# A memory-attention layer rebuilt: denominators from segment sums, query divided first, heads on column tiles

## What is computed

```python
def step(carry, inp):                       # over 8 segments of L = 32 tokens, per sequence and head (H = 8, DK = DV = 64)
    mem, z = carry                          # start: zeros, and ones / DK
    q_s, k_s, v_s = inp
    sq = elu(q_s) + 1.0
    att_mem = sq @ mem / (sq @ z)
    sk = elu(k_s) + 1.0
    mem = mem + einsum('bhlk,bhlv->bhkv', sk, v_s)
    z = z + sk.sum(over the segment's tokens)
    att_dot = softmax(q_s @ k_s.T * DK ** -0.5)     # within the segment
    att = gate * att_mem + (1.0 - gate) * (att_dot @ v_s)
    return (mem, z), att
s = att @ Wo
h = gelu(xn @ W_fc_ternary.T); h = layernorm(h) * ln_w + ln_b       # 512 features
g = h @ W_proj_ternary.T
x = x + s * silu(g)
```

## Time and profile before

| | |
|---|---|
| median of 3 runs | 3093.98 us (3093.51 to 3094.66) |
| the profiled execution | 3093.26 us; its span, from the first to the last instruction, 3091.5 us |
| busy in the span | PE 2651.5 us (86%), DVE 2365.2 (77%), ACT 1580.9 (51%), POOL 318.3 (10%) |
| mean granted TensorE clock | 0.864 of 2.4 GHz |
| layer 0, first to last update of x | 110.2 to 655.9 us |

### The profile page before, as it was taken

One profiled execution on the slowest core, in us unless ns is written; L12 is line 12 of the kernel. 1 busy time (PEld: TensorE's weight loads), 2 busy tenths in 40 slices (PEclk: granted clock), 3 DMA queues, 4 the chain that ended last, 5 costly groups with the idle time before them and its releaser, 6 DMA issues. The chain is left out here.

```text
span 3091.5 us, 56965 instructions
## 1 busy us (share of the span) xinstructions
PE 2651.5 (86%) x19564; PEld 2068.0 (67%) x19564; DVE 2365.2 (77%) x6278; ACT 1580.9 (51%) x3260; POOL 318.3 (10%) x340
## 2 busy tenths in 40 slices
PE   1999999979999999987764898888888889888887
PEld 1888887867777777765553666656666666656665
DVE  2777777768878888868526788888888888888887
ACT  1333334336555666555333556566565556556554
POOL 0000000000000000003321111111111111111111
PEclk9999999989999999989785777777778777777777
DMA  7000000000000000011021344323334344323334
GB/s 210 1 0 0 0 0 0 0 0 1 1 1 1 1 1 0 1 32 55 26 58 61 90 103 103 88 76 85 94 85 104 93 100 103 96 76 81 91 85 114
DMA packets 86520, 163.69 MB, mean 53 GB/s; under 512 B 18856, under 2 KB 45616, under 8 KB 86320
## 3 DMA queue, kind: packets, MB, share of 16 engines
q0 software_dynamic: 20480, 62.93, 10.7%
q1 hardware_dynamic: 64640, 98.15, 9.8%
q10 hardware_dynamic: 1200, 0.27, 0.1%
HBM read 92.60 MB, written 9.99 MB: 33 GB/s over the span
## 5 line engine op out<-in xcount | busy, mean ns | idle before, releaser
L1104 ACT ACTIVATE b_neg<-b_neg,b_nmax 128x128 f32<-128x128 f32 (+1 forms) x512 | 190.9, 443 | 207.9 <-DVE b_nmax L1258 207.9
L2770 DVE TENSOR_TENSOR_SCAN d_state<-w,d_state 128x1024 f32<-128x1024 f32 x128 | 291.0, 2284 | 6.2 <-issue 5.9
L2507 ACT ACTIVATE d_probs<-l_bank,w_b 128x256 f32<-128x256 f32 x512 | 210.7, 469 | 155.8 <-PE l_bank L2345 153.3
L2345 PE MATMUL l_bank<-xnT,w_w 128*128 128x256 f32 x1024 | 245.1, 382 | 14.0 <-ACT d_probs L2507 14.0
L2356 PEld LDWEIGHTS l_bank<-w_w,d_probs 128*128 128x128 f32 x2048 | 244.9, 192 | 11.7 <-ACT d_probs L2507 5.3
L2356 PE MATMUL l_bank<-w_w,d_probs 128*128 128x128 f32 x2048 | 252.7, 276 | 0.0
L2275 PE MATMUL l_bank<-w 9*128 9x256 f32 x1040 | 208.3, 669 | 25.6 <-ACT w L2430 18.9
L2469 ACT ACTIVATE w<-d_delta,d_negA 128x255 f32<-128x255 f32 x520 | 220.3, 499 | 0.0
L96 POOL TENSOR_TENSOR ln_rstd<-ln_var_eps,minus_half 128x2 f32<-128x2 f32 x50 | 63.9, 1278 | 1482.2 <-DVE ln_var_eps L90 1482.2
L2345 PEld LDWEIGHTS l_bank<-xnT,w_w 128*128 128x128 f32 x1024 | 184.7, 190 | 40.7 <-ACT d_probs L2507 20.9
L2275 PEld LDWEIGHTS l_bank<-w 9*128 9x128 f32 x1040 | 123.3, 320 | 96.0 <-issue 32.3
(11 more groups left out here) (404 smaller groups left out, 6110.2 us busy)
## 6 DMA issues: line engine op xcount, KB each, us to landing
d_bct<-l_bc SPq DMA_DIRECT2D x132, 512.0 KB, 3.9
d_state<-d_state POOLq DMA_DIRECT2D x96, 512.0 KB, 6.5
d_state<-d_state POOLq DMA_DIRECT2D x32, 256.0 KB, 3.8
x_sorted<-x SPq DMA_DIRECT2D x1, 2560.0 KB, 16.5
w<-in_L_ffn_w_dram SPq DMA_DIRECT2D x1, 2048.0 KB, 9.4
w_w<-in_L_ffn_W_dram SPq DMA_DIRECT2D x1, 2048.0 KB
c2e_xg<-x_sorted SPq DMA_DIRECT2D x16, 128.0 KB, 2.3
y_sorted<-c2e_yo SPq DMA_DIRECT2D x16, 128.0 KB, 1.8
```

Of the source, the lines that this page charges most:

```text
L1104: done = nc.scalar.activation(neg[:, slot, cols], neg[:, slot, cols], ACT.Exp, bias=nmax[:, slot, a:a + 1], scale=-1.0)
L2345: done = nc.tensor.matmul(bank[:, b, i * T:(i + 1) * T], w.w1[:, e, k * P:(k + 1) * P], x1T[:, :], start=True, stop=True)
L2507: done = v.activation(hid[:, e % 2, k, :], bank[:, b, i * T:(i + 1) * T], ACT.Gelu, bias=w.b1[:, e, k:k + 1])
L2770: done = v.tensor_tensor_scan(group, dA[i][:, g % (NG - 1), :, :].rearrange("p m t -> p (m t)"), group, 0.0, ALU.mult, ALU.add)
```

## The change

Only `layer0` and its constants are touched.

- Denominators: VectorE sums the positive keys over each segment (`tensor_reduce`), a scan adds the segments up from 1/64 (`tensor_tensor_scan`), the positive queries are multiplied by that sum, and TensorE sums over the 64 features of each head with a block matrix of ones (`denominators`). ScalarE inverts: Ln, then Exp of the negative (`invert`). VectorE divides the positive queries by it (`share_q`) ahead of the memory's scores. The scores, thus the output, are then divided already. `zrow`, the ones column, `share_memory` and `combine` go.
- Softmax: the probabilities are divided by their sum before they are transposed.
- Memory's scores are computed for both heads of a pair next to each other on two 64-row tiles; one mask instruction of 2 x 384 columns covers both.
- Output: `heads_out` takes values as the stationary operand (64 columns of the array per head, the two heads of a pair on the two column tiles) and scores or probabilities as the moving one, and sums memory's and softmax's parts in one bank, already transposed. `turn_attention` goes.
- Work on other engines: q and k are clipped on ScalarE (relu of -x, from PSUM); the hidden layer's normalisation moves from VectorE to ScalarE (`apply_norm`), with one more GpSimd product for its bias.
- ScalarE's function tables are loaded by hand: gelu with tanh, and exp with ln, in turn; four loads per iteration.
- `pos`, `vdot`, `vmem` and `xnT` get two buffers, the loop runs over pairs of sequences, and the values, the sums and the divided queries of sequence n+1 are made in iteration n.

The new parts, cut: the denominators, the scores and the output, the order of TensorE's loop body, and two parts of ScalarE. In that order `hidden` waits for `shifted_ready`, `turn_hidden` for the normalised hidden layer.

```diff
+            def denominators(m, half):
+                pe.wait_ge(qz_ready, 2 * m + half + 1)
...
+                for i in range(2):
+                    done = nc.tensor.matmul(bank[:, DEN, i * T:(i + 1) * T], c.head_block[:, :], qz[:, 2 * half + i, :],
+                                            start=True, stop=True)
...
+            def memory_scores(n, par, j):
+                pe.wait_ge(posq_ready, 2 * n + j // 2 + 1)
+                pe.wait_ge(mem_masked, NCH0 * n + j + 1)
+                for lo, keys in ((0, slice(0, P)), (P, slice(P, T))):
+                    for odd in range(2):
+                        rows = slice(DK0 * odd, DK0 * odd + DK0)
+                        done = nc.tensor.matmul(bank[:, MEM + odd, 2 * lo:2 * lo + T - lo], pos[rows, par, j, 1, keys],
+                                                pos[rows, par, j, 0, lo:], start=True, stop=True,
+                                                tile_position=(DK0 * odd, 0))
...
+            def heads_out(n, par, j):
+                if j == 0:
+                    pe.wait_ge(probs_ready, n + 1)
+                    pe.wait_ge(v_taken, TILES * n + TILES)
+                if j % 2 == 0:
+                    pe.wait_ge(attT_copied, 2 * n + j // 2 + 1)
+                pe.wait_ge(mem_masked, NCH0 * n + j + 2)
+                cols = slice(j % 2 * T, j % 2 * T + T)
+                for step in range(4):
+                    for odd in range(2):
+                        hd = 2 * j + odd
+                        out = bank[DK0 * odd:DK0 * (odd + 1), OUT, cols]
+                        v = slice(hd * DK0, (hd + 1) * DK0)
+                        if step == 0:
+                            left, right = vmem[:, par, 0, v], memT[:, j % 2, odd, 0:T]
+                        elif step == 1:
+                            left, right, out = vmem[:, par, 1, v], memT[:, j % 2, odd, T:], out[:, P:]
+                        else:
+                            a = step - 2
+                            left, right = vdot[:, par, a, v], probsT[:, odd, a * (H0 // 2) + j, :]
+                            out = out[:, a * P:(a + 1) * P]
+                        done = nc.tensor.matmul(out, left, right, start=(step == 0), stop=(step == 3),
+                                                tile_position=(0, DK0 * odd))
...
+                    memory_scores(n, par, 0)
+                    own_scores()
+                    memory_scores(n, par, 1)
+                    for a in range(TILES):
+                        hidden(n, par, a)
+                    turn_x(n + 1)
+                    project_qk(n + 1, 1 - par, 0)
+                    project_qk(n + 1, 1 - par, 1)
+                    project_qk(n + 1, 1 - par, 2)
+                    project_qk(n + 1, 1 - par, 3)
+                    heads_out(n, par, 0)
+                    memory_scores(n, par, 2)
+                    for a in range(TILES):
+                        turn_hidden(n, a)
+                    heads_out(n, par, 1)
+                    memory_scores(n, par, 3)
+                    for a in range(TILES):
+                        project_v(n + 1, 1 - par, a)
+                    denominators(n + 1, 0)
+                    heads_out(n, par, 2)
+                    heads_out(n, par, 3)
+                    denominators(n + 1, 1)
+                    for a in range(TILES):
+                        project_out(n, a)
...
             def copy_qk(m, j):
+                v.activation(low[:, j, :], bank[:, j % 2, :], ACT.Relu, scale=-1.0)
+                v.activation(qk[:, j, :, :].rearrange("p a t -> p (a t)"), bank[:, j % 2, :], ACT.Copy)\
+                    .then_inc(qk_taken, 1)
+                v.drain()
+                v.activation(low[:, j, :], low[:, j, :], ACT.Exp, scale=-1.0).then_inc(low_exp, 1)
+            def invert(m, half):
+                v.activation(lden[:, half, :], bank[:, DEN, :], ACT.Ln).then_inc(ln_done, 1)
...
+                v.activation(rden[:, :, :].rearrange("p i t -> p (i t)"), lden[:, half, :], ACT.Exp, scale=-1.0).then_inc(rden_ready, 1)
```

More of the change, by code:

```diff
@@ new lines, in share_q, with take_v @@
+            def share_q(m, par, half):
+                pairs = slice(2 * half, 2 * half + 2)
+                dve.wait_ge(rden_ready, 2 * m + half + 1)
+                v.tensor_tensor(pos[:, par, pairs, 0, :], pos[:, par, pairs, 0, :], rden[:, :, :], ALU.mult)\
+                    .then_inc(posq_ready, 1)
+            def take_v(m, par, a):
+                dve.wait_ge(v_in_psum, TILES * m + a + 1)
+                if a == 0 and later(m - 1):
+                    dve.wait_ge(out_done, NCH0 * m)
+                v.tensor_tensor(vdot[:, par, a, :], bank[:, a, :], c.gate1m[:, :], ALU.mult)
+                v.tensor_tensor(vmem[:, par, a, :], bank[:, a, :], c.gate[:, :], ALU.mult).then_inc(v_taken, 1)
@@ L716, in _ @@
+            v.memset(probsT[:, :, :, :].rearrange("p o g k -> p (o g k)"), 0.0)
+            v.memset(zsum[:, :, 0:1], 1.0 / DK0)
+            v.memset(keep[:, :, :], 1.0)
+            v.drain()
+            v.memset(keep[:, :, 0:1], 0.0)
             dve.wait_ge(c.x_loaded, 16)
@@ new lines, in _ @@
+                    elu_plus_1(n + 1, 1 - par, 2)
+                    elu_plus_1(n + 1, 1 - par, 3)
+                    for a in range(TILES):
+                        take_v(n + 1, 1 - par, a)
+                    times_z(n + 1, 1 - par, 1)
+                    share_q(n + 1, 1 - par, 0)
+                    share_q(n + 1, 1 - par, 1)
+                    for a in range(TILES):
+                        dve.wait_ge(th_ready, TILES * n + a + 1)
+                        v.scalar_tensor_tensor(out=u[:, a, :], in0=th[:, a, :], scalar=1.0, in1=bank[:, ROW + a, 0:D],
+                                               op0=ALU.add, op1=ALU.mult)
+                        v.drain()
+                        v.scalar_tensor_tensor(out=u[:, a, :], in0=u[:, a, :], scalar=0.5,
+                                               in1=bank[:, ROW + a, D:2 * D], op0=ALU.mult, op1=ALU.mult)\
+                            .then_inc(sz_taken, 1)
@@ L761, in combine @@
                     v.drain()
                     for a in range(TILES):
-                        done = v.tensor_tensor(att[:, a, lo:lo + HALF0 * DK0].rearrange("p (h v) -> p h v", v=DK0),
-                                               part[:, half, a, :, :], part2[:, a, :, :], ALU.add)
-                    if half == 1:
-                        done.then_inc(att_ready, 1)
-                    v.drain()
-                for a in range(TILES):
-                    take_v(a)
-                mask_memory(0)
@@ L824, in _ @@
[L824 to L826 removed]
+                        v.tensor_tensor(c.x[:, 2 * n + a, :], c.x[:, 2 * n + a, :], u[:, a, :], ALU.add)
 def layer1(nc, c):
```

566 lines of the change are left out of this document (245 added, 321 removed).

## The result

The changed kernel takes 3067.55 us (median of 4 runs, 3066.7 to 3069.1) against 3093.86 us for the kernel before (4 runs, 3093.51 to 3094.66): 0.9911 of it, 95% interval 0.9899 to 0.9923. Forecast were 3060 and the range 3005 to 3100. The profiled execution took 3067.96 us with a span of 3065.1.

What follows compares the result with a forecast made beforehand. TensorE was taken as the bound before, the chain between engines after. 3093.98 us, less 35.6 for 15 iterations going from 36.37 to 34.0 us, plus 1.9 at the start, gave 3060.3; range 3005 to 3100.

Steps and rivals of the forecast that it cites:

- The forecast chain: Step-by-step order of the four engines through one layer0 iteration: 31.7 us at full clock, 34.0 with the clock's fall.
- the standstill: TensorE idle from 2.2 to 5.4 us of the iteration, 3.2 us, waiting for VectorE's mask 0 before memory_scores(1).
- The clock: TensorE's granted clock falls after its idle wait in most iterations, doubling the products that follow: +2.3 us per iteration.
- The chain at full clock: One layer0 iteration with TensorE's clock up, from second gating product to the next: 31.7 us against 36.37 before.
- The unmeasured forms: Instructions without a row in the profile, such as the pool's new multiply, 0.1 to 0.7 us, taken as 0.7.
- The ground of the fall: TensorE's clock falls after standing still 3.18 us, seen in the third layer, and stays at 1.00 after 1.91 us.
- The start: Work before layer0's loop: first iteration ends at 111.9 instead of 110.0 us, +1.9 us.
- The clock stays up: Rival: TensorE keeps full clock in layer0's loop, 31.7 us per iteration, 3023 us in all; chance 0.22.
- The clock stays down for the whole iteration: Rival: once fallen, TensorE's clock stays low through the layer0 iteration, 44 us each, 3222 us in all; chance 0.14.
- Columns one after the other: Rival: heads_out's two column tiles run serially, +1.07 us per call for (0) and (1), 37.1 us, 3110; chance 0.05.
- Loads with a drain: Rival: ScalarE's table loads carry a drain of about 1.38 us, 36.1 us per iteration, 3094 us; chance 0.02.
- Handovers dearer by 1 to 2 us: Rival: handovers between engines and unmeasured forms cost another 1 to 2 us, 3075 to 3090 us; chance 0.10.

Runs made afterwards that it cites:

- e1_fill: Changed kernel plus four products nobody reads on TensorE per iteration, between own scores and memory_scores(1): 3040.36 us, ratio 0.9823.
- e12_fill_more_masks: e5_more_masks plus two 512-column products nobody reads on TensorE before memory_scores(3): 3013.11 us, ratio 0.9730.
- e3_serial_columns: Changed kernel with the loops of heads_out exchanged, all steps of one head before the other's: 3095.22 us, ratio 1.0001.
- e6_two_loads: Changed kernel plus two ScalarE table loads per iteration, to the gelu set and back to exp, behind the copy of xnT: 3122.65 us, ratio 1.0083.
- e5_more_masks: Changed kernel with hidden products ahead of memory_scores(1), four masked-score buffers instead of two, memory_scores(2), (3) and mask 2 moved earlier: 3015.82 us, ratio 0.9737.
- e11_mask_first: e5_more_masks with mask 2 moved ahead of the hidden layer's statistics on VectorE: 3017.62 us, ratio 0.9753.
- e8_before_pairs: Kernel before the change, with only memory's scores of a head pair issued together on two 64-row tiles: 3058.53 us, ratio 0.9876.

## Why the prediction was right, and where its terms were off

The forecast chain held step by step. Measured against 318.03, with the forecast in brackets, the clock's 2.3 us already in it from project_qk 3 on:

- Mask 0 ends at 5.41 (5.4), the standstill is 3.30 us (3.2), the mask itself 956 ns (955).
- project_qk 3 ends at 16.6 (14.4 + 2.3 = 16.7), the probabilities at 14.2 (14.0): not a tie once the clock is down; the projections are last.
- heads_out(0) ends at 17.8 (15.65 + 2.3 = 17.95).
- The iteration ends at 34.1 (34.0).

Two terms were off against each other, and that the period came out within 0.15 us is in part luck. **The clock** costs 2.0 us per iteration, not 2.3: pair 1's scores cost 0.73 more and the two hidden tiles 1.25, together 1.98, and e1_fill, the same order, takes 32.2 us where its clock stays up, 1.95 less. turn_x was already back at full clock (0.38 us), where I had it doubled. **The chain at full clock** is 32.2 us, not 31.7. In an iteration of e1_fill without a fall (time 0 at 209.73) project_qk 3 ends at 14.8 for 14.4, mask 2 at 18.0 for 17.5, the second denominators at 27.7 for 27.0, the iteration at 32.2 for 31.7. No single instruction carries the excess; that 0.05 us for each handover was too little is argued. The unmeasured forms were no part of it: scan 0.20, GpSimd's multiply 0.20 (taken as 0.7, hidden either way). apply_norm, at 1.50 us instead of 1.1, lay beside the chain. The busy times per iteration were 26.5 us for TensorE (some 23 forecast, at full clock), 24.6 for VectorE (26.1) and 22.2 for ScalarE (22.9).

**The ground of the fall** was too simple. I set a standstill of 3.18 us that had a fall against one of 1.91 that had none. For this order it came true, and e1_fill bears it out, but the length of the standstill isn't what decides: in the profile above the clock falls half a microsecond into it, and in e12_fill_more_masks it fell in every iteration with no standstill over 1.2 us, less than the 1.91 that had none. What decides, no run isolates.

**The start** costs 2.9 us, not 1.9. The stretches view of after ahead of the loop shows what the forecast left out:

```profile
71.60:78.40 6.80, 4.57 (x9) 2.52 (x8) 3.65 (x7) 2.45 (x4) 0.00 (x0) 0.51 0.00 0
```

The denominators' waits are holes as well (2.1 and 2.2 us), the clock falls there too, project_v takes 3.20 us for 1.98, and the loop's scores start at 79.05 instead of 77.9.

**The giveback** of 4 us in later layers was not in the sum. It is most of what separates 3060 from 3067.55: 1.0 at the start, 15 x 0.15 = 2.2 in the period, 4 behind it.

**The rivals.** The clock stays up (3023): refuted by the stretch at 0.51, though e1_fill shows that its premise would have been worth 27 us. The clock stays down for the whole iteration (3222): refuted, it is back after 6.8 us. Columns one after the other (3110): not the case, and e3_serial_columns measured that case at 3095: a pair's output costs 0.7 us more (1.94 against 1.24) and not 1.07, and the period grew by 1.7 us and not by 3.1. Loads with a drain (3094): refuted by rows of e6_two_loads. By the Trainium skill's page "ScalarE: Activation LUTs" (section "What ACT_TABLE_LOAD costs") the three loads in a row would hold three drains of 1.38 us; the trace has none. Handovers dearer by 1 to 2 us (3075 to 3090): true by half a microsecond. The chances of same and slower, 0.05 and 0.16, don't add up from the rivals' own, which give 0.02 and 0.19.

So the large change moved the time by no more than 0.9%, for two reasons that the runs separate. It took TensorE from bound to 78% busy, but left a chain through VectorE's masks that takes 32.2 us in that order. And it opened the hole that halves the clock. Both are matters of order and buffers: e5_more_masks, with the same computation, is 52 us faster than the change.

## What to carry to other kernels

- When an engine stops being the bound, read its new idle stretches and not its busy sum. A hole of TensorE that costs nothing by itself can bring the clock down for what follows: here 2.0 us per hole of 3.3 us. Fill it by moving independent work into it, ahead of the waiting instruction, and then look where the clock falls now: e12_fill_more_masks filled a hole and kept a fall in every iteration.
- Price a fall of the clock by iterations of one trace, those with it against those without, and not by the mean clock: e11_mask_first won 5% of clock and no time, because its order cost what the clock gave.
- Try the parts of a large rewrite alone first. One reordering in the old kernel (e8_before_pairs) was worth 38 us, more than the rewrite as it was first ordered.

## What was not expected of the hardware

- A delay of 0.51 us per iteration on ScalarE cost 4 us in all, the next 0.51 us cost 33: with a wait of TensorE of 1.36 us before project_qk 2 a second fall of the clock follows in two of three iterations, with one of 0.84 us in none.
- The clock fell in every iteration of e12_fill_more_masks, where TensorE never stood still for more than 1.2 us; a standstill of 2.13 us in an iteration of e5_more_masks went by without one.
- Column tiles of 64 overlap only when their records alternate (1.9 us against 1.24), row tiles of 64 in either order.
- A table load of the set already loaded isn't in the trace at all.
